# Six attention and feed-forward layers on one core: another order of the pieces of POOL, ACT, DVE and PE, and a mask in parts of 64 rows by 32 columns

## What is computed

```python
def shift_tokens(t):
    a, s = jnp.split(t, 2, -1)
    s = jnp.pad(s, ((0, 0), (1, 0), (0, 0)))[:, :-1]
    return jnp.concatenate([a, s], -1)
...
q = l2norm(q) * qs
k = l2norm(k) * ksc
q = q * cos * scale + rotate_half(q) * sin * scale
k = k * cos * inv + rotate_half(k) * sin * inv
...
mask = (it < jb) | (it > jb + w) | (jb == -1)
sim = jnp.einsum('bhwie,bhwje->bhwij', bq, bk2) * QK_SCALE
sim = jnp.where(mask, -jnp.finfo(sim.dtype).max, sim)
attn = jax.nn.softmax(sim, -1)
out = jnp.einsum('bhwij,bhwje->bhwie', attn, bv2)
...
return a * jax.nn.gelu(gate, approximate=False) @ W2 + b2
...
for i in range(DEPTH):
    x = attn_layer(shift_tokens(x), Wqkv[i], q_scale[i], k_scale[i], Wo[i]) + x
    x = ffn_layer(shift_tokens(x), ln_g[i], ln_b[i], W1[i], b1[i], W2[i], b2[i]) + x
```

## Time and profile before

| | us |
|---|---|
| median of 3 runs (4387.13 to 4396.32) | 4388.52 |
| profiled execution, device time | 4396.54 |
| its span | 4394.5 |
| PE busy (88%) | 3877.8 |
| DVE busy (75%) | 3301.3 |
| ACT busy (65%) | 2866.7 |
| POOL busy (54%) | 2381.0 |
| PE weight loads (62%) | 2704.7 |

### The profile page before, as it was taken

The page is one execution under the profiler, slowest core; times in us unless marked ns, Lnnn a source line. Parts: engine busy times, 40 slices in busy tenths (PEclk is TensorE's granted clock), DMA queues, the critical chain, the costliest instruction groups (busy, mean ns, idle before and its releaser), DMA issues. The chain is left out here.

```text
span 4394.5 us, 158126 instructions
## 1 busy us (share of the span) xinstructions
PE 3877.8 (88%) x69264; PEld 2704.7 (62%) x69456; DVE 3301.3 (75%) x4767; ACT 2866.7 (65%) x4676; POOL 2381.0 (54%) x1968
## 2 busy tenths in 40 slices
PE   5999999868888898988888898889889989998987
PEld 2222222357767777776767677767777776777775
DVE  7899999567777777777777777777777777777774
ACT  2588888656666666666666666666666666666664
POOL 2100000176666666666666666666666666667673
PEclk7899999989999999999999999999999999999998
DMA  3010000033333333333333333333333333333331
GB/s 98 16 52 20 20 20 16 18 100 92 90 92 90 98 104 97 90 92 90 103 90 93 93 103 102 91 92 90 92 96 97 98 90 99 108 93 93 93 101 52
DMA packets 202479, 358.82 MB, mean 82 GB/s; under 512 B 35518, under 2 KB 74050, under 8 KB 201538
## 3 DMA queue, kind: packets, MB, share of 16 engines
q1 hardware_dynamic: 201794, 348.71, 28.8%
HBM read 236.68 MB, written 111.67 MB: 79 GB/s over the span
## 5 line engine op out<-in xcount | busy, mean ns | idle before, releaser
L1120 POOL TENSOR_TENSOR T<-T 128x1024 f32<-128x1024 f32 x384 | 905.2, 2379 | 99.1 <-DVE T L1578 98.8
L1138 POOL TENSOR_TENSOR T<-T,rn 128x1024 f32<-128x1024 f32 x384 | 723.6, 1905 | 0.3
L1205 PE MATMUL PA<-Wqkv,XS 128*128 128x512 f32 x2304 | 654.5, 419 | 43.4 <-DVE XS L1539 40.1
L705 ACT ACTIVATE E<-p_s 128x512 f32<-128x512 f32 x1024 | 555.8, 596 | 168.9 <-PE p_s L565 163.9
L639 DVE TENSOR_REDUCE negmax<-p_max 128x1 f32<-128x1024 f32 x512 | 605.6, 1221 | 51.5 <-PE p_max L545 38.0
L1573 DVE TENSOR_TENSOR T<-PA,tab 128x1024 f32<-128x1024 f32 x192 | 235.2, 1225 | 415.4 <-ACT SQ L1411 415.4
L1205 PEld LDWEIGHTS PA<-Wqkv,XS 128*128 128x128 f32 x2304 | 410.3, 190 | 162.9 <-DVE XS L1539 48.8
L1230 PE MATMUL PD<-ident,T 128*128 128x128 f32 x3072 | 423.2, 281 | 86.5 <-POOL T L1138 44.0
L1411 ACT ACTIVATE SQ<-PA 128x1024 f32<-128x1024 f32 x192 | 197.1, 1027 | 404.9 <-PE PA L1205 404.4
L1114 POOL TENSOR_TENSOR Ew<-Ew,sm 128x1024 f32<-128x1024 f32 x192 | 365.8, 1905 | 155.4 <-DVE sm L1562 155.4
L1586 DVE TENSOR_REDUCE ss<-SQ 128x32 f32<-128x2048 f32 x192 | 437.0, 2276 | 0.0
(11 more groups left out here) (168 smaller groups left out, 7068.5 us busy)
## 6 DMA issues: line engine op xcount, KB each, us to landing
VW<-v_rows SPq DMA_DIRECT2D x768, 256.0 KB, 4.5
v_rows<-Vs SPq DMA_DIRECT2D x192, 512.0 KB, 6.0
Wraw<-in_Wqkv SPq DMA_DIRECT2D x40, 192.0 KB, 5.8
QA<-parts_q SPq DMA_DIRECT2D x384, 16.0 KB
KA<-parts_k SPq DMA_DIRECT2D x192, 32.0 KB
parts_q<-parts SPq DMA_DIRECT2D x8, 384.0 KB, 2.6
parts_k<-parts SPq DMA_DIRECT2D x8, 384.0 KB, 2.7
Wo<-in_Wo SPq DMA_DIRECT2D x12, 256.0 KB, 5.9
```

Source lines behind the costliest of these rows:

```text
L705: act.activation(E[:, s % 4, c, :], p_s[:, i % 2, :], ACT.Exp, scale=DH ** -0.5)\
L1120: pool.tensor_tensor(out=t_, in0=t_, in1=T2[:, i * HALF:(i + 1) * HALF], op=ALU.add).then_inc(ad.sem, 1)
L1138: pool.tensor_tensor(out=t_, in0=t_, in1=rn[:, p, i * LH:(i + 1) * LH].unsqueeze(2).broadcast_to([P, LH, LD]), op=ALU.mult).then_inc(no.se ...
L1205: mm = pe.matmul(pair[:, half, :], XS[:, b, i, 1:P + 1], Wqkv[:, l % 2, j, lo:lo + 512], start=(k == 0), stop=(k == 2))
```

## The change

All in `layers`, but for the mask's table.

- PE: `attend` moves from behind `project_v` and `input_T` to right behind the k transposes; `project_v` comes after `input_T` and, in d = 3, after `ff_shift`. `ff_tokens` comes after `project_v`. Gate 1 follows gate 0 in d = 1, gate 2 goes to the next slot (d = 2) between the projections of q and k; value 2 goes to d = 3, in the same place; values 0 and 1 and `ff_norm` come after `project_v`; `ff_down` comes after `output`.
- POOL: its slots are numbered one later (tile s - 1 where it was s). In a slot stand norms, normalise q, divide, normalise k, add q, add k, and no longer normalise twice, add twice, norms, divide. Divide is for tile s - 3 counted as on PE, it was s - 2. The split of the weights stands between the two additions, in d = 2 as counted on PE (it was d = 3), and the table likewise, in d = 0.
- DVE: `sums` (now of s - 3) and `output` (s - 4) open the slot, before the rotations; `input_T` comes before the FF pieces; the three values are parted like on PE.
- ACT: gate 0 stands at the end of d = 1, gate 1 and gate 2 in d = 2 around the first square; `ff_norm` opens d = 1; `halo_k` comes after ET; `project_v` after OT; roots before exponentials; the split in d = 2.
- The mask: 8 matmuls of 64 rows by 32 columns in place of 2 of 128 by 128, each with 512 columns of moving data as before. The mask of a window that has a predecessor is now taken for windows 1 to 3 of the first tile.
- PE waits for the split of the weights only at the first step of a layer.

```diff
-LAST_SLOT = TILES + 2 * B + 1
+LAST_SLOT = TILES + 3 * B
...
@@ -1156,26 +1156,25 @@ on_pool
-            if d == 0 and is_step(u - 3) and u - 3 >= last * NT:
-                result(u - 3)
+            if is_tile(s - 2):
+                norms(s - 2)
+                normalise(s - 2, 0)
+            if is_tile(s - 4):
+                divide(s - 4)
+            if is_tile(s - 2):
+                normalise(s - 2, 1)
             if is_tile(s - 1):
-                normalise(s - 1, 0)
-            if is_tile(s - 1):
-                normalise(s - 1, 1)
-            if is_tile(s):
-                rotate(s, 0)
-            if is_tile(s):
-                rotate(s, 1)
-            if d == 3 and u < last * NT:
+                rotate(s - 1, 0)
+            if d == 3 and 0 <= u < last * NT:
                 split_next(u)
-            if d == 3 and is_step(u - 1):
-                frs_power(u - 1)
             if d == 1 and is_step(u + 1):
                 rotary_table(u + 1)
-            if is_tile(s):
-                norms(s)
-            if is_tile(s - 2):
-                divide(s - 2)
+            if is_tile(s - 1):
+                rotate(s - 1, 1)
+            if d == 0 and is_step(u - 2):
+                frs_power(u - 2)
+            if d == 2 and is_step(u - 3) and u - 3 >= last * NT:
+                result(u - 3)
...
-                if b == 0 and 0 < u <= last * NT:
+                if b == 0 and u % NT == 0 and u > 0:
                     pe.wait_ge(wsp.sem, wsp.at(u - 1))
...
-            for par in range(2):
-                pe.matmul(PC[:, par, :], ident_b[:, :], mask[:, min(t, 1), :], start=True, stop=False,
-                          skip_group_check=True)
+            for v in range(NW):
+                for par in range(2):
+                    o, q = par * LD, v * WIN
+                    pe.matmul(PC[q:q + WIN, par, :], ident_b[o:o + LD, o:o + WIN], mask[o:o + LD, min(t + v, 1), :],
+                              start=True, stop=False, skip_group_check=True)
...
@@ -1643,29 +1645,30 @@ on_dve
+            if is_tile(s - 3):
+                sums(s - 3)
+            if is_tile(s - 4):
+                output(s - 4)
+            if d == 3 and is_step(u - 2):
+                ff_value(u - 2, 2)
             if is_tile(s):
                 rotate(s, 0)
...
+            if is_tile(s + 1):
+                input_T(s + 1)
             if d == 3 and is_step(u - 1):
                 ff_tokens(u - 1)
                 ff_stats(u - 1)
                 ff_scale(u - 1)
-            if is_tile(s + 1):
-                input_T(s + 1)
-            if is_tile(s - 2):
-                sums(s - 2)
+            if d == 2 and is_step(u - 2):
+                ff_value(u - 2, 0)
+                ff_value(u - 2, 1)
             if d == 3 and is_step(u - 2):
                 ff_down(u - 2)
-            if is_tile(s - 3):
-                output(s - 3)
...
-    m[0:WIN, 0, :, 0:WIN] = MASKED
+    m[:, 0, :, 0:WIN] = MASKED
```

More of the change, by code:

```diff
@@ L1353, in on_pe @@
                 transpose_qk(s - 1, 1)
[L1354 to L1359, removed]
+            if is_tile(s - 3):
+                attend(s - 3)
             if is_tile(s + 1):
@@ L1362, in on_pe @@
             if d == 3 and is_step(u - 1):
-                ff_tokens(u - 1)
-            if is_tile(s - 3):
-                attend(s - 3)
+                ff_shift(u - 1)
+            if is_tile(s):
+                project_v(s)
+            if d == 2 and is_step(u - 2):
+                ff_value(u - 2, 0)
+            if d == 1 and is_step(u - 2):
+                ff_gate(u - 2, 0)
             if d == 0 and is_step(u - 2):
@@ L1368, in on_pe @@
             if d == 1 and is_step(u - 2):
-                ff_gate(u - 2, 0)
+                ff_gate(u - 2, 1)
+            if d == 3 and is_step(u - 1):
+                ff_tokens(u - 1)
             if d == 2 and is_step(u - 2):
                 ff_value(u - 2, 1)
+            if is_tile(s - 3):
+                output(s - 3)
             if d == 3 and is_step(u - 2):
                 ff_down(u - 2)
[L1374 to L1378, removed]
-                output(s - 3)
-            if d == 1 and is_step(u - 2):
-                ff_gate(u - 2, 2)
     def on_act(act):
@@ L1499, in on_act @@
             u, d = divmod(s, B)
+            if d == 2 and is_step(u - 2):
+                ff_gate(u - 2, 1)
+            if d == 1 and is_step(u - 2):
+                ff_norm(u - 2)
             if is_tile(s):
                 square(s, 0)
+            if d == 2 and is_step(u - 2):
+                ff_gate(u - 2, 2)
             if is_tile(s):
                 square(s, 1)
-            if is_tile(s - 1):
-                halo_k(s - 1)
             if is_tile(s - 1):
@@ L1514, in on_act @@
                 ff_shift(u - 1)
+            if is_tile(s - 3):
+                attend(s - 3)
+            if d == 2 and 0 <= u < last * NT:
+                split_next(u)
             if is_tile(s):
                 project_v(s)
-            if is_tile(s + 1):
-                input_T(s + 1)
-            if is_tile(s - 3):
-                attend(s - 3)
-            if d == 3 and u < last * NT:
-                split_next(u)
+                roots(s)
             if is_tile(s - 2):
                 exponentials(s - 2)
-            if is_tile(s):
-                roots(s)
             if d == 1 and is_step(u - 2):
-                for i in range(NCH):
-                    ff_gate(u - 2, i)
-            if d == 0 and is_step(u - 2):
-                ff_norm(u - 2)
+                ff_gate(u - 2, 0)
     def on_dve(dve):
@@ L1653, in on_dve @@
                 norms(s)
-            if d == 2 and is_step(u - 2):
-                for i in range(NCH):
-                    ff_value(u - 2, i)
+            if is_tile(s + 1):
+                input_T(s + 1)
             if d == 3 and is_step(u - 1):
```

8 lines of the change are left out of this document (6 added, 2 removed).

## The result

The changed kernel takes 4224.11 us (median of 4 runs, 4221.2 to 4235.41) against 4392.25 for the kernel before beside it (4387.13 to 4396.32): ratio 0.9623, interval 0.96 to 0.9645. It is faster, by 168 us where 278 were forecast, and lies above the range (4050 to 4205). The profiled execution took 4221.2. One execution of the last experiment (6057 us, at a granted clock of 0.82) was in a slower state than all others here, and its time is left out.

The account below looks back on a forecast made before the run. PE was taken as the bound, though not full. 6.7 us per step times 46 gave 308, plus 3 for filling and draining, less 33 for pauses: 278 off 4396.5, so 4118.5 us; range 4050 to 4205.

Parts of the forecast that it names:

- The timetable: Layer slots on PE, each moved piece checked against when it is wanted: 6.7 us less per quiet step, 308 over 46.
- the forecast place: Slot d=3 on PE: waits of 0.2 to 0.5 us for FS and OT, there only.
- The mask: Before the scores on PE: eight small matmuls take 0.30 us instead of 0.45, saving 0.15 per tile.
- the optimistic end: Mask on PE: the favourable end of its estimate, 0.24 us saved per tile.
- The table load: ACT in d=2: 1.28 us without further drain; the skill's 1.38 more would cost 50 us in all.
- The step that failed: PE's pauses without a releaser: stay at 60 to 80 us; up to 38 us more come out, 33 taken.
- Rival 2: Mask's pieces on PE run in turn, 1.70 us instead of 0.30: 269 us lost, 4379; chance 0.04.
- rival 1: New lags on DVE and POOL too short: 0.7 us lost per slot, 129 us, 4240; chance 0.09.
- rival 3: k or attend waits over 1.2 us mid-slot, PE returns at lower clock: 497 us lost, 4575; chance 0.04.

Follow-up runs that it names:

- the last experiment: Attend in 32 matmuls of 64 columns instead of 64 of 32, against the changed kernel (output not the reference's): 3940.95 us, ratio 0.8966 to the kernel before.

## Why the prediction was wrong, point by point

**The timetable was right for a quiet step.** Slots now begin at 2055.35 (d=1), 2070.13 (d=2), 2085.87 (d=3), 2105.01 (d=0) and 2118.78: lengths 14.78, 15.74, 19.14 and 13.77, where 15.2, 16.0, 18.9 and 14.1 were forecast. The sum is 63.43 against 64.0 taken, so the gain of a quiet step was 7.31 and not 6.7, 28 us more over 46 steps. Waits for XS, G and Ew are gone, qT is 42.0 (40 to 50 forecast), FS 10.4 in 40 steps and OT 20.5 in 42, 0.26 and 0.5 each, in the forecast place. POOL is busy 47.24 of 63.43 us, over 70%. The granted clock was 1.00 in the quiet step and 0.969 over the whole span, for 0.976. One difference: normalise 1 in d=3 makes k wait 0.76 at 2094.03, not 0.15. The mean step, forecast at 65 to 66 us, is 68.17.

**The mask** saved more in a quiet slot than forecast, and nothing in the end. It takes 0.22 us (2058.31 to 2058.53) where 0.30 were taken. From the start of the k projection to the scores it is 1.70 us after (2056.83 to 2058.53) and was 1.94:

```profile
2041.16 1.56 PE L1205 MATMUL PB<-Wqkv,XS 128*128 128x512 f32 x6
...
2043.10 1.48 PE L1246 MATMUL PC<-kT,qT 64*32 64x64 f32 x128
```

So 0.24 per tile, the optimistic end. The 0.24 us for the eight that the prediction estimated by the Trainium skill ("TensorE: Matmul & The Clock Gate", Measured speedup vs the span model) is near the 0.22 of the trace. But a kernel with the old mask takes as long: the six more matmuls per tile pay in pauses what they save.

**The table load** adds no drain here either, 1.28 us and the next square 0.02 later:

```profile
2073.65 1.28 ACT L1490 ACT_TABLE_LOAD   x1
2074.95 1.03 ACT L1412 ACTIVATE SQ<-PB 128x1024 f32<-128x1024 f32 x1
```

The Trainium skill's further 1.38 us ("ScalarE: Activation LUTs", What ACT_TABLE_LOAD costs) does not show.

**The step that failed** is the one of the pauses: "With those waits gone up to 38 more come out; I take 33", and behind it "pauses with no releaser still at 60 to 80 us". They are 178 us. The term let them cost 55 + 33 = 88 us in the steps, measured are 218: 130 too few, less the 28 of the quiet step, which leaves the 102 us by which the profiled execution (4221.2) missed its forecast (4118.5). The fault was to carry the pauses over as a fixed sum. They were read as something that lies over the kernel; they come from PE using up a piece of its program before the next is there, and a change that brings 64 short matmuls nearer to 64 others and takes out the waits between changes that. The six matmuls more per tile have a small part in it: with the old mask 130 of the 163.5 us in 3000 stay. The two groups of the earlier trace rows and the two torn ones of the earlier trace rows stood at just the two dense places.

**The rivals.** Rival 2 (mask in turn) and 3 (a pause in mid-slot at the cost of the clock) did not come, and rival 1 (lags too short) neither: the transposes of q and k wait for POOL 15.3 us in all. Its 4240 is near the time only by chance. What rival 3 said of PE coming back slower holds behind the pauses at the borders: the granted clock of 0.68 behind the pause of 1.80, and 1.28 us of step for each us of pause.

**How the gain is made up.** No piece can be priced alone. Taken back one at a time from the changed kernel, POOL's order costs 135 us, attend's place 181 with input_T covered and 382 without; set alone into the kernel before, attend's place costs 333. These sum to more than the 168 gained: read from the waits of these runs, PE, ACT and POOL form one ring, and each piece is worth something only where the other engines have the matching order.

**What stays open.** That a pause is PE waiting for its next 256 instructions rests on the distances, the number of packets, the times at which packets land, and the run with half of attend. What is not shown is what sets the start of a fetch. Mostly it comes 0.9 us after the border before, but behind a border with a pause 4.4 us in the median, in the changed kernel. A rule from the time of the last two pieces did not fit (the scores cut in two), and idle time at the q transposes (130.6 us) did not help. How the traffic of V delays a piece was not followed either; leaving it out takes away 20 us of the 178 in the changed kernel, and other traffic was not tried. A correct attend in 32 matmuls (both halves of a head pair against weights laid out with zeros between) wasn't tried; it would probably need a second copy on ACT, which stands on the ring. No version that gives the reference's values was faster than the changed kernel.

## What to carry to other kernels

When waits are taken out of an engine that issues many short instructions, look at its pauses without a releaser first: count the records from one to the next, and if they are multiples of one number, take them for the supply of the program, look at the packets of the instruction queue beside them, and do not carry their sum over to a tighter schedule. Here fewer and longer instructions at the densest place took away 283 us, more than the whole new order did, and a trick that saves 0.24 us by six more instructions was worth nothing. A timetable laid over the trace, slot by slot, gave each slot within 0.5 us; the mean over many steps beside the quiet step tells what it leaves out.

## What had not been expected of the hardware

- PE stops at borders of 256 instructions of the program for up to 2.7 us, 178 us in all in the changed kernel and 70 before; with 12,288 of 70,608 matmul records fewer, 36.1 us in 3000 instead of 163.5.
- PE goes on 1.2 to 1.7 us after the packet with its next instructions has landed, some 2.4 us after that packet began; attend and the scores use up a piece in less.
- In the kernel before, leaving out V's loads and stores took the pauses from 70 to 23 us: the data transfers have a part in when the program comes. How is not shown.
- Attend's 64 columns in a matmul instead of 32 cost little: 64 records in 1.2 us against 128 in 2.0, about 18 and 15.6 ns each. Between these two sizes PE's time goes by the number of matmuls, hardly by their columns.
